# Macaron attention: values products behind the scores, the output's addition between the two rotations, table load and copies reordered

## What is computed

```python
h = shift_token(x)                       # half of the features moved by one token
q, k, v = split(h @ wqkv)                # 8 heads of 64
q = l2norm(q) * qs;  k = l2norm(k) * ks
q, k = rotary_xpos(q, k)                 # x * cos-table + swapped(x) * sin-table
sim = q @ k^T  (window 64 and the one before it, masked)
x = x + (softmax(sim) @ v) @ wo
h = layernorm(shift_token(x)); a, g = split(h @ w1 + b1)
x = x + (a * gelu(g)) @ w2 + b2
```

## Time and profile before

| | us |
|---|---|
| median of 3 runs (range) | 2209.62 (2207.27 to 2210.42) |
| the profiled execution, own time | 2207.21 |
| its span, first to last instruction | 2205.4 |
| TensorE busy | 1849.2 (84%) |
| VectorE busy | 1575.7 (71%) |
| ScalarE busy | 1392.0 (63%) |
| GpSimd busy | 1286.6 (58%) |
| mean granted TensorE clock, share of full | 0.924 |

### The profile page before, as it was taken

One profiled execution on the slowest core, in us unless ns is written; L12 is line 12 of the kernel. 1 busy time (PEld: TensorE's weight loads), 2 busy tenths in 40 slices (PEclk: granted clock), 3 DMA queues, 4 the chain that ended last, 5 costly groups with the idle time before them and its releaser, 6 DMA issues. The chain is left out here.

```text
span 2205.4 us, 52050 instructions
## 1 busy us (share of the span) xinstructions
PE 1849.2 (84%) x16960; PEld 1410.0 (64%) x16961; DVE 1575.7 (71%) x2848; ACT 1392.0 (63%) x3948; POOL 1286.6 (58%) x1099
## 2 busy tenths in 40 slices
PE   4269956626996599999999999675999999999996
PEld 4158832415884377777777776342777777777774
DVE  4658858554885588878788886243788888788872
ACT  5135533212554488788878887364787888878873
POOL 4354410246441688878788785101887878788771
PEclk9989969658997799999999999787999999999998
DMA  6212140022214111111110110000111011111111
GB/s 204 67 60 64 41 122 0 22 74 65 61 44 128 58 28 26 24 24 26 26 28 20 26 25 16 4 0 5 31 26 26 20 28 26 23 27 23 22 23 39
DMA packets 87309, 88.28 MB, mean 40 GB/s; under 512 B 13978, under 2 KB 65863, under 8 KB 87016
## 3 DMA queue, kind: packets, MB, share of 16 engines
q1 hardware_dynamic: 77288, 68.09, 12.3%
q0 software_dynamic: 8704, 17.85, 2.4%
q10 hardware_dynamic: 1152, 0.25, 0.1%
HBM read 35.60 MB, written 22.22 MB: 26 GB/s over the span
## 5 line engine op out<-in xcount | busy, mean ns | idle before, releaser
L2040 POOL TENSOR_TENSOR mac_probs<-mac_probs,mac_prec 128x512 f32<-128x512 f32 x256 | 265.5, 1043 | 199.5 <-DVE mac_prec L1855 198.6
L1716 ACT ACTIVATE mac_probs<-banks,mac_nmax 128x128 f32<-128x128 f32 x1024 | 359.6, 386 | 0.0
L2020 POOL TENSOR_TENSOR route_pool<-route_pool 128x1024 f32<-128x1024 f32 x128 | 303.5, 2371 | 35.7 <-issue 13.1
L1812 DVE TENSOR_TENSOR route_pool<-banks,tables 128x1024 f32<-128x1024 f32 x256 | 300.7, 1214 | 33.2 <-ACT route_pool L1676 27.8
L1846 DVE TENSOR_REDUCE mac_nmax<-banks 128x4 f32<-128x512 f32 x256 | 164.8, 686 | 126.2 <-PE banks L1544 126.2
L2031 POOL TENSOR_TENSOR mac_qkn<-route_pool,mac_rc 128x1024 f32<-128x1024 f32 x128 | 243.9, 1906 | 15.8 <-issue 7.6
L854 POOL DMA_INDIRECT x_sorted<-route_pool,route_index x128 | 124.5, 973 | 216.3 <-DVE route_index L666 122.0
L862 POOL DMA_INDIRECT y_tokens<-moe_bench,moe_goal x144 | 141.0, 979 | 173.0 <-DVE moe_bench L805 123.7
L1716 ACT ACTIVATION_READ_ACCUMULATOR mac_probs<-banks,mac_nmax 128x1 f32 x1024 | 231.8, 226 | 0.0
L54 PE MATMUL banks<-wqkv_h,mac_hh 128*128 128x512 f32 x384 | 179.2, 467 | 27.4 <-POOL mac_hl L1995 22.4
L388 PE MATMUL banks<-w,moe_gh 128*128 x576 | 159.6, 354 | 46.9 <-issue 30.9
(11 more groups left out here) (315 smaller groups left out, 5086.9 us busy)
## 6 DMA issues: line engine op xcount, KB each, us to landing
mac_v_even<-mac_v SPq DMA_DIRECT2D x224, 128.0 KB, 2.2
moe_xs<-x_sorted SPq DMA_DIRECT2D x144, 72.0 KB
route_pool<-y_tokens SPq DMA_DIRECT2D x16, 512.0 KB, 7.2
y_tokens<-moe_bench,moe_goal POOLq DMA_INDIRECT x144, 2.3
moe_bench<-in_L_attn_x SPq DMA_DIRECT2D x8, 256.0 KB, 5.2
route_pool<-in_L_ffn_W SPq DMA_DIRECT2D x4, 512.0 KB, 6.8
x_sorted<-route_pool,route_index POOLq DMA_INDIRECT x128
b<-in_b_flat SPq DMA_DIRECT2D x1, 2048.0 KB
```

The source lines that it names most:

```text
L1716: e = act.activation(probs[:, r, p, :], m.ps[:, S + r, p * P:(p + 1) * P], ACT.Exp, bias=nmax[:, r, p:p + 1], accum_out=psum[:, r, p:p + 1])
L1812: turn = dve.tensor_tensor(turned[:, i, :, :].rearrange("q k (h s j) -> q k h s j", s=2, j=DH // 2), q[:, :, :, ::-1, :] if i else q, tabl ...
L2020: pool.tensor_tensor(sums[:], turned[:, 0, :, :], turned[:, 1, :, :], ALU.add).then_inc(added, 1)
L2040: pool.tensor_tensor(probs[:, r, :, :], probs[:, r, :, :], prec[:, r, :].unsqueeze(2).to_broadcast([P, HP, P]), ALU.mult).then_inc(shared[ ...
```

## The change

TensorE's list takes `values(n-1)` directly behind `sims(n)`, and projects values first, keys and queries after it (`centre` in B and `up` in D then stand ahead of the keys' projection). ScalarE loads the Gelu table ahead of `square`, and does `exps(n+1,1)` ahead of `keep_kt(n+2)`. VectorE copies the queries behind `norms` and `reciprocals(n,1)`, and does `add_out` between the two multiplications of `rotate`. GpSimd does `f_take` behind `add(n+3)` rather than ahead of it, with a wait for that sum; the wait for the split input moves from the keys' to the values' projection, and the wait ahead of overwriting it from the values' to the keys' and queries' count.

```diff
 # TensorE
                 if which == 2:
+                    if t % 2 == 0:
+                        pe.wait_ge(split, START + 2 * j + t // 2 + 1)
                     pe.wait_ge(v_kept, START + k)
...
-                if which == 1 and t % 2 == 0:
-                    pe.wait_ge(split, START + 2 * j + t // 2 + 1)
...
                     sims(n, t)
+                    values(n - 1, *before)
                     turn_qk(n + 1, (t + 1) % NT)
                     if t == 0:
                         up(i - 2, lay, 0, 2, F, gated, MC * (i - 2) + 1)
                     if t == 2:
                         down(i - 2, lay)
-                    values(n - 1, *before)
-                    project(n + 3, *ahead, lay, 1)
+                    project(n + 3, *ahead, lay, 2)
                     if t == 1:
                         centre(i - 1)
                     if t == 3:
                         up(i - 1, lay, 0, 0, F, gelued, MC * (i - 1) + 1)
+                    project(n + 3, *ahead, lay, 1)
                     project(n + 3, *ahead, lay, 0)
-                    project(n + 3, *ahead, lay, 2)
                     turn_probs(n, 1)
 # ScalarE
                     scale(n + 2)
-                    square(n + 3)
                     if t == 2 and there(i - 1):
                         act.preload_act_table_set(GELU)
+                    square(n + 3)
...
+                    exps(n + 1, 1)
                     keep_kt(n + 2, (t + 2) % NT)
-                    exps(n + 1, 1)
 # VectorE: rotate(k, j, t, lay, i) now issues its i-th multiplication alone
                     maxima(n, 0)
-                    keep_qt(n + 1)
                     norms(n + 2)
                     reciprocals(n, 1)
+                    keep_qt(n + 1)
...
-                    rotate(n + 3, *ahead, lay)
+                    rotate(n + 3, *ahead, lay, 0)
                     add_out(n - 1, *before, lay)
+                    rotate(n + 3, *ahead, lay, 1)
                     maxima(n + 1, 1)
 # GpSimd
-                    pool.wait_ge(v_projected, START + NT * (j - 1) + 2 * (s + 1))
+                    pool.wait_ge(qk_projected, START + 2 * (NT * (j - 1) + 2 * (s + 1)))
...
-            def settle(n):
+            def settle(n, summed):
...
+                if live(summed):
+                    pool.wait_ge(added, START + summed + 1)
...
                     norm(n + 2, (t + 2) % NT)
-                    if t == 0 and there(i - 1):
-                        settle(n)
-                        if there(i + 1):
-                            pool.wait_ge(split, START + 2 * (i + 1) + 1)
-                        f_take(i - 1, lay)
                     if t == 2 and there(i + 2):
-                        settle(n)
+                        settle(n, n + 2)
...
                     if t == 3:
                         upper(i + 2, 0)
                     add(n + 3)
+                    if t == 0 and there(i - 1):
+                        settle(n, n + 3)
+                        if there(i + 1):
+                            pool.wait_ge(split, START + 2 * (i + 1) + 1)
+                        f_take(i - 1, lay)
```

More of the change, by code:

```diff
@@ L1801, in _, with rotate @@
         def _(dve):
-            def rotate(k, j, t, lay):
+            def rotate(k, j, t, lay, i):
                 if not live(k):
@@ L1806, in rotate @@
                 w = ws[layer(j, lay)]
[L1807 to L1815, removed]
+                if i == 0:
+                    dve.wait_ge(squared, START + k + 1)
+                    dve.wait_ge(added, START + k)
+                q = m.ps[:, A:A + 2, :].rearrange("q k (h s j) -> q k h s j", s=2, j=DH // 2)
+                table = w.tables[:, t, i::2, :].rearrange("q k (s j) -> q k s j", s=2)
+                turn = dve.tensor_tensor(turned[:, i, :, :].rearrange("q k (h s j) -> q k h s j", s=2, j=DH // 2),
+                                         q[:, :, :, ::-1, :] if i else q,
+                                         table.unsqueeze(2).to_broadcast([P, 2, NHD, 2, DH // 2]), ALU.mult)
+                if i == 1:
+                    turn.then_inc(rotated, 1)
             def norms(k):
```

## The result

The changed kernel takes 2265.8 us (median of 4 runs, 2258.0 to 2268.1) against 2209.0 us for the kernel before (median of 4 runs, 2207.3 to 2210.4): ratio 1.0249, 95% interval 1.0226 to 1.0272. It is slower by 57 us. The forecast was slower by 32 us with a range up to 2262: right in sign and in the place, too small in size, and outside the range.

The account below looks back on a forecast made before the run. TensorE's list order was taken to bound the items, with A at the softmax chain. Late copies (+1.6 us per item) less savings gave 16.0 us per application, twice 32: 2241.6 us, 1.4% slower; own range 2213 to 2260, 8-in-10 range 2206 to 2262.

Parts of the forecast that it names:

- What bounds the kernel: Macaron item's four steps: TensorE's list order bounds B, C and D; A is already at the four-engine softmax chain.
- Part 1: TensorE, values directly behind scores: three array shape changes per step instead of four, saving 0.2 us, bounds 0 to 0.35.
- the 2246 us: Whole-kernel time if one drain of four goes at near 0.1 us, half the 0.2 us saving taken per step.
- Part 2: C, values projected first and Gelu table ahead of squares: 0.4 us gained in layer 0, nothing in layer 1.
- Part 3: ScalarE, exponentials ahead of keys' copy: second group ends 0.18 us later, A from 8.38 to 8.58 us.
- Part 4: VectorE, output addition between the rotation's multiplications: costs the chain 0.1 us at most, nothing on TensorE.
- Part 5: GpSimd's copies behind the addition: `centre` in B waits until 14.15 us after A's start, +1.6 us per item.
- The clock rival: Gap ahead of `centre` halves TensorE's clock: up to 1.7 us more in each of 30 items, 2290 us; chance 0.09 with table rival.
- The prediction's own sign of being wrong: TensorE's clock rows: the forecast is wrong if they show 0.50 inside the items.
- Its upper bound: Range's upper end: +1.85 us per item from the late copies with nothing saved, giving +50 us.

Follow-up runs that it names:

- experiment 11: Kernel of experiment 1 with the new order only in B, D and layer 0's C, table load and values' projection early in each C: 2108.3 us, ratio 0.9892.
- experiment 1: Changed kernel with one edit undone, GpSimd's two shifted copies (f_take) ahead of the addition again: 2128.6 us against 2134.0 for the kernel before, ratio 0.9978.
- experiment 9: Kernel before with only C's part: values projected first and the Gelu table loaded ahead of the squares: 2197.8 us, ratio 0.9953.
- experiment 7: Kernel of experiment 1 with ScalarE's keys' copy ahead of the exponentials again: 2288.3 us, ratio 1.0363 to the kernel before.
- experiment 8: Kernel of experiment 1 with the output added behind both rotation multiplications again: 2217.6 us against 2208.1 for the kernel before, ratio 1.0047.
- experiment 4: Changed kernel with its hardware loops written out on all engines: 2171.4 us, ratio 1.0184 to the kernel before.
- experiments 7 to 10: experiment 7, experiment 8, experiment 9 and a fourth: experiment 1's kernel, old order in A, output added behind both multiplications in A and D; fourth 2199.8 us, ratio 0.9960.
- e11_longer_gap: Kernel of experiment 4 with one more small GpSimd copy and its wait ahead of the two shifted copies: 2202.7 us, ratio 1.0337 to the kernel before.

## Why the prediction was off, point by point

**What bounds the kernel** held. A is at the softmax chain and the other steps at TensorE's list; experiment 11, which treats them accordingly, gets the gain that follows from it.

**Part 1, values behind the scores: right in size, by a reading that was in part wrong.** From the first score product to the second matmul of the first projection, B has 0.97 + 1.08 + 0.86 + 0.31 = 3.22 us in the rows above (1014.33 to 1017.55). Before, the same stretch was scores to transposes 0.97, transposes 1.02, values 1.08 and the first two projection matmuls 0.34: 3.41. The saving is 0.19, D and the unheld B of experiment 1 show 0.17 to 0.2, forecast 0.2. Nearly all of it is the transposes' 1.02, which became 0.86. Rows of the kernel before, timeline of PE, in A and in B:

```profile
993.04 0.39 PE L55 MATMUL banks<-mac_fh,w_l 128*113 128x512 f32 x1
...
1002.15 0.50 PE L54 MATMUL banks<-wqkv_h,mac_hh 128*128 128x512 f32 x1
1002.49 0.39 PE L55 MATMUL banks<-wqkv_h,mac_hl 128*128 128x512 f32 x1
```

The prediction read the 0.34 us from the first to the second matmul of a projection behind values as 0.11 us more than the usual 0.23, and put a single change of shape near 0.1. But `up` behind the transposes, with no change of shape, has 0.31 there as well (992.73 to 993.04), so only 0.03 of it came with the change. The one price that the rows give for a change is the 0.17 us of the transposes, and that is about what a step saves.
The Trainium skill, page "TensorEngine Tiling (Array Packing)", Tiling Modes, says that changing the mode drains the engine; by that rule one of four drains goes. The trace agrees, with 0.97 us from scores to values as from scores to transposes, and 0.17 to 0.2 us saved per step; the 2246 us that the prediction drew from the rule rested on its 0.1.

**Part 2, table and projection in C: right in layer 0** (11.86 against 11.9; its part of the gain, 0.4 us, stands alone in experiment 9), slightly short in layer 1. There C is 12.51 in the one item written out and 12.63 in loops, against 12.5 forecast; in item 12 `output` (L1582) waits for VectorE's copy, as the prediction said:

```profile
1276.76 1.16 PE L1582 MATMUL banks<-mac_ot,wo 128*128 128x128 f32 x8 [0.53 <-DVE mac_ot L1864]
```

**Part 3, the keys' copy: right** (A 8.55 against 8.58), and experiment 7 shows that its alternative costs 85 us.

**Part 4, the addition in the middle: right but for layer 1's C,** which is 0.2 us shorter without it (experiment 8). Leaving it out costs 15 us in all.

**Part 5, the copies behind the addition: the mechanism was right and its size was not.** This is the step that failed: "So C starts at 14.15 + 4.98 = 19.1 after A instead of 17.47: +1.6 per item". With A's 0.2 taken off, it is +1.4 for each B, 39.2 us in all; measured are 55.6. Three parts make up the 16.4 us between them.

- For the 12 items written out it is nearly right. C starts 14.17 + 5.07 = 19.24 after A, and B grew by 1.59 instead of 1.4: 2.2 us.
- The other 16 run inside hardware loops, where the gap is 1.91 us and not 1.53. There B, without a fall of the clock, grew from 9.20 to 11.08, 0.49 more than the 1.4: 7.8 us. I had worked the latencies out of an item written out and applied them to all; the kernel before gave a hint, since its B is 9.2 in loops and 9.1 outside.
- In 4 of these 16 the clock fell behind the gap: 4 x 1.6 = 6.4 us.

With the loops written out (experiment 4), B's total is +42.7 where 39.2 was forecast.

**The clock rival** was named with the right price, up to 1.7 us where 1.6 was measured. It was put at "every item" and given little weight since "the shorter gap is what I expect". It came in 4 items, all in loops, where the gap was longer than expected. The prediction's own sign of being wrong, 0.50 in the clock rows inside the items, is there in those four.

**The rest**, 9 us net, was in no term: 7.5 us outside the steps, 1.5 in item 0 (its first step waits 2.1 us for a rotation that was not in flight yet), 1.6 in layer 1's C and 0.5 each in D and layer 0's C, less 2.4 in A and at the end. That the 7.5 belong to the change isn't shown: the part ahead of the macaron phase, which no kernel here touches, was 5 to 9 us longer than in the first profile in the four kernels of experiments 7 to 10, on another chip.

The range stopped at 2262. Its upper bound took +1.85 for an item's A and B together and no fall of the clock; the loop items had +2.05, and the falls came on top.

## What to carry to other kernels

An in-order list turns a late input into idle time exactly where its reader stands, so of a moved producer ask first what its new predecessor waits for: here an addition that waited for a rotation. Decide reorderings per step by what bounds that step; the order that gives 0.2 us to a step full of matrix work took 0.17 from one bound by a chain through four engines. And take latencies from the copy of the code that runs most often, a loop body has its own.

## What the runs showed of the hardware that was not expected

- Waits inside a hardware loop, where the count comes from a register, end later: 0.49 instead of 0.30 us for the run of waits between two GpSimd operations, 0.14 instead of 0.06 us from GpSimd to TensorE. With the loops written out the difference is gone (gap 1.51 us in every item of `e7_unrolled`); that it is the register isn't shown.
- TensorE's clock can go from 2.4 to 1.2 GHz for 3.41 us behind a single idle gap of 1.87 to 1.95 us in a step that is otherwise full: 14 of 44 did, and none of the 40 of 1.51 to 1.53 us. Each fall costs 1.6 us here, about as much as the gap itself. In `e11_longer_gap` the gap grew by 0.36 us in 28 items; B became 10 us longer by that and 16 us longer by ten falls.
- Loading the other activation table ahead of the squares needs no further load: the squares run under the Gelu table, with 32 loads of each of the two tables before and after, and 3948 instructions on ScalarE in both.
